# Transposing normalised tokens before their scale is known, with unused TensorE products between the stages

## What is computed

```python
def act_qdq(x):                       # one scale for the whole tensor
    scale = jnp.maximum(jnp.max(jnp.abs(x)) / qmax, 1e-12)
    return jnp.clip(jnp.round(x / scale), -qmax - 1.0, qmax) * scale

x = x + tanh(g_xattn[0]) * cross_attention(layernorm(x), ctx)      # "x2" below
h = layernorm(x)
h = act_qdq(h)
up, gate = act_qdq(h @ Wup.T), act_qdq(h @ Wgate.T)
sig  = fixed_qdq_u16(sigmoid(gate))
gate = act_qdq(gate * sig)
o    = act_qdq(gate * up)
x    = x + tanh(g_ffn[0]) * (o @ Wdown.T)
```

## Time and profile before

| | us |
|---|---|
| median of 3 runs | 591.79 (590.91 to 591.95) |
| the profiled execution's own time | 594.23 |
| its span in the trace | 592.1 |
| attention ends on PE | 432.2 |
| input maximum known (DVE reciprocal L1358) | 440.1 |
| first gate product | 445.6 |
| last gate tile copied out | 484.7 |
| all second-pass products done | 548.1 |
| first and last down product | 552.5 and 589.4 |

### The profile page before, as it was taken

How to read it: one execution, slowest core, us unless ns; L and a number is a source line. 1 busy time by engine, 2 the same in 40 slices (tenths; PEclk the granted TensorE clock), 3 DMA queues, 4 the chain that set the end, 5 groups by cost and what they waited for, 6 DMA issues and landing times. The chain is left out here.

```text
span 592.1 us, 10973 instructions
## 1 busy us (share of the span) xinstructions
PE 522.1 (88%) x3921; PEld 455.9 (77%) x3921; DVE 410.9 (69%) x1080; ACT 298.1 (50%) x859; POOL 123.4 (21%) x137
## 2 busy tenths in 40 slices
PE   2999999999999999999999999998738999900798
PEld 2888889888988988888898898886527888700698
DVE  4679844755674574576457458758676998999896
ACT  2734622543443353264335336426515559989992
POOL 3001310220231031022013012212223008940000
PEclk9999999999999999999999999999967999955699
DMA  7922001100110110110011001004000100010033
GB/s 248 359 105 73 1 1 54 37 2 19 35 35 0 53 35 0 53 35 0 0 53 35 0 2 37 2 1 159 2 18 1 38 0 1 0 35 1 1 106 107
DMA packets 18478, 25.86 MB, mean 44 GB/s; under 512 B 1216, under 2 KB 15808, under 8 KB 18448
## 3 DMA queue, kind: packets, MB, share of 16 engines
q1 hardware_dynamic: 18192, 25.17, 12.7%
q0 software_dynamic: 256, 0.30, 0.3%
HBM read 21.27 MB, written 4.19 MB: 43 GB/s over the span
## 5 line engine op out<-in xcount | busy, mean ns | idle before, releaser
L805 ACT ACTIVATE probs<-bank,nmax 128x129 f32<-128x129 f32 x256 | 90.7, 367 | 118.0 <-DVE nmax L1133 117.8
L1552 POOL TENSOR_TENSOR probs<-probs,rinv 128x512 f32<-128x512 f32 x64 | 66.6, 1041 | 338.8 <-DVE rinv L1141 338.8
L608 PE MATMUL bank<-wv,ctxT 128*128 128x512 f32 x384 | 94.3, 397 | 0.0
L600 PE MATMUL bank<-ctxT,wk 128*128 128x256 f32 x672 | 88.9, 282 | 0.0
L600 PEld LDWEIGHTS bank<-ctxT,wk 128*128 128x128 f32 x672 | 83.6, 188 | 0.0
L608 PEld LDWEIGHTS bank<-wv,ctxT 128*128 128x128 f32 x384 | 70.5, 188 | 16.9 <-issue 1.2
L1145 DVE COPY pT<-bank 128x512 f32<-128x512 f32 x64 | 43.7, 683 | 20.8 <-PE bank L671 18.7
L786 ACT ACTIVATE oT<-bank 128x256 fp32r<-128x256 f32 x64 | 24.7, 385 | 60.0 <-PE bank L680 60.0
L600 PE MATMUL bank<-xnT,wq 128*128 128x256 f32 x336 | 54.7, 298 | 0.0
L805 ACT ACTIVATION_READ_ACCUMULATOR probs<-bank,nmax 128x1 f32 x256 | 52.0, 203 | 0.0
L600 PEld LDWEIGHTS bank<-xnT,wq 128*128 128x128 f32 x336 | 43.2, 188 | 7.2 <-issue 1.2
(11 more groups left out here) (170 smaller groups left out, 814.6 us busy)
## 6 DMA issues: line engine op xcount, KB each, us to landing
craw<-in_ctx SPq DMA_DIRECT2D x8, 512.0 KB, 3.3
stage<-in_L_xattn_Wkv SPq DMA_DIRECT2D x8, 512.0 KB, 12.6
xa<-in_x SPq DMA_DIRECT2D x8, 256.0 KB, 2.7
xr<-in_x SPq DMA_DIRECT2D x8, 256.0 KB, 2.8
x_scratch<-y SPq DMA_DIRECT2D x7, 256.0 KB, 2.1
x2all<-x_scratch SPq DMA_DIRECT2D x1, 1792.0 KB, 7.8
xres<-x_scratch SPq DMA_DIRECT2D x6, 256.0 KB, 2.9
out<-yout SPq DMA_DIRECT2D x6, 256.0 KB, 2.2
```

Of the source, the lines that this page charges most:

```text
L600: last = mm(bk[:, n * TG:(n + 1) * TG], wt[a][:, k, f], act_t[b][:, k, :], start=(k == 0 and i == 0), stop=(k == kk - 1 and i == len(TERMS ...
L608: last = mm(bk[:, :], ctxT[a][:, k, b * S:(b + 1) * S], wv[w][:, k, h * 512:(h + 1) * 512], start=(k == 0 and i == 0), stop=(k == KC - 1 a ...
L805: last = nc.scalar.activation(probs[:, c % 2, u, 0:NK], score_bank[c % 2][h][:, b * QW:b * QW + NK], ACT.Exp, bias=nmax[:, c % 2, u:u + 1] ...
L1552: G.tensor_tensor(probs[:, c % 2, :, 0:S], probs[:, c % 2, :, 0:S], rinv[:, c % 2, :].rearrange("p (u o) -> p u o", o=1).to_broadcast([P, ...
```

## The change

- A first square root covers the 14 batches that are known before the last group ends (`root(0)`, started by DVE in the last attention unit F8), and a second one only the last two. There are now four roots instead of three.
- ACT normalises the tokens, x * (1/deviation) - mean/deviation, pair by pair, between the roots (`x_normalise`, pairs 0 to 6; pair 7 in the gate pass). PE transposes these normalised tokens, pairs 0 to 5 before the scale is known, each into a bank of its own (`x_bank`), pairs 6 and 7 after the first quarter of the gate pass.
- With the scale known, the transposed tokens are multiplied by its reciprocal straight out of the bank into int16: pairs 0 and 1 by DVE, the rest by ACT (`x_integers`). `fa[2]`, `x_float` and POOL's rounding are gone. The high part is made from the int16 tile. The low part of pairs 2 to 7 moves from DVE to POOL, for which ACT writes one more f32 copy (`xfloat`).
- DVE takes gate maxima and minima over two tiles at a time (`gate_range`).
- PE runs products whose results nobody reads (`keep_awake`, 128x512, into bank 7): 4 before `global_max(0)`, 7 after it; 4 after each of the products 4 to 11 of the second pass; 8 after `global_max(4)`.
- In the second pass DVE rounds chunk 7 instead of chunk 11.
- SP's read of the residuals waits for the last transposition instead of POOL's last rounding.

```diff
+            def keep_awake(count, rows, spare_bank):
+
+                for _ in range(count):
+                    mm(spare_bank[:, :], rows[:, 0:P], rows, start=True, stop=True)
...
             def x_transposes(t):
-                pe.wait_ge(xf_ready, t + 1)
-                if t >= 2:
-                    pe.wait_ge(xt_lo, t - 1)
+                last_pair = t == NT // 2 - 1
+                pe.wait_ge(xn2_ready, t + 1)
+                if t == 5:
+                    pe.wait_ge(x2_ready, NG)
+                if last_pair:
+                    pe.wait_ge(xi_scalar, 3)
...
+            for t in range(NT // 2 - 2):
+                x_transposes(t)
+            pe.wait_ge(x2_ready, NG + 1)
+            keep_awake(4, wg[0][:, 0, 0:512], bank[7])
             global_max(0)
-            for t in range(2):
-                x_transposes(t)
+            keep_awake(7, wg[0][:, 0, 0:512], bank[7])
...
-                        if m == 0 and tg == 0 and j in (1, 3):
-                            x_transposes(2 + j // 2)
...
-                    if m == 0 and tg < 2:
-                        x_transposes(2 * tg + 4)
-                        x_transposes(2 * tg + 5)
-            for n in range(2, 5):
+                    if m == 0 and tg == 0:
+                        x_transposes(NT // 2 - 2)
+                        x_transposes(NT // 2 - 1)
+            for n in range(2, 4):
                 global_max(n)
+            for q in range(4, NCH):
+                pe.wait_ge(o_ready, q)
+                keep_awake(4, down_rows, bank[7])
+            global_max(4)
+            keep_awake(8, down_rows, bank[7])
...
+            def x_normalise(t):
+                last_pair = t == NT // 2 - 1
+                if t == 0:
+                    act.wait_ge(x2all_in, 16)
+                if t == 0 or last_pair:
+                    act.wait_ge(xaffine, 2 if last_pair else 1)
+                for b in range(2):
+                    n = 2 * t + b
+                    last = nc.scalar.activation(xnlast[:, b, :] if last_pair else x2all[:, n, :], x2all[:, n, :],
+                                                ACT.Identity, bias=fa[:, 3, n:n + 1], scale=rs3[:, 0, n:n + 1])
+                last.then_inc(xn2_ready, 1)
+
+            root(0)
+            x_normalise(0)
+            root(1)
+            for t in range(1, 4):
+                x_normalise(t)
+            root(2)
+            for t in range(4, 6):
+                x_normalise(t)
+            root(3)
+            x_normalise(6)
...
             def x_high(t):
-                act.wait_ge(xt_done, t + 1)
-                high(xT[0][:, :, t * TG:(t + 1) * TG],
-                     unit_bank[t % 2][:, :].rearrange("p (k s) -> p k s", k=KD)).then_inc(xt_hi, 1)
+                if t < 2:
+                    act.wait_ge(xi_vector, t + 1)
+                else:
+                    act.wait_ge(xi_scalar, t - 1)
+                    high(xfloat(t), xi[:, t % 4, :, :])
+                high(xT[0][:, :, t * TG:(t + 1) * TG], xi[:, t % 4, :, :]).then_inc(xt_hi, 1)
...
+            x_high(0)
+            x_high(1)
+            x_integers(2)
+            x_integers(3)
+            x_high(2)
+            x_high(3)
+            for n in range(4 * KI):
+                gu(0, n)
+                if n in (1, 2, 7, 8):
+                    t = {1: 4, 2: 5, 7: 6, 8: 7}[n]
+                    x_integers(t)
+                    x_high(t)
+                if n == 3:
+                    x_normalise(NT // 2 - 1)
...
             link(V.reciprocal(s1(5), s1(4)))
-            link(V.tensor_scalar(fa[:, 2, :], rs3[:, 0, :], s1(5), None, ALU.mult))
...
-            V.memset(pause[:, :], 0.0).then_inc(xaffine, 1)
...
+            for t in range(2):
+                dve.wait_ge(xt_done, t + 1)
+                V.tensor_scalar(xi[:, t, :, :], x_bank[t][:, :].rearrange("p (k s) -> p k s", k=KD), s1(5), None,
+                                ALU.mult).then_inc(xi_vector, 1)
+            x_offsets(slice(known, NT))
...
+            def gate_range(n):
+
                 tg, j = n // KI, n % KI
...
+                dve.wait_ge(gu_out, n + 2)
+                src = gate[:, j:j + 2, tg * 512:(tg + 1) * 512]
+                V.tensor_reduce(amax[:, 0, n:n + 2], src, AX.X, ALU.max)
+                return V.tensor_reduce(amax[:, 0, 4 * KI + n:4 * KI + n + 2], src, AX.X, ALU.min, negate=True)
...
+            for t in range(2, NT // 2):
+                pool.wait_ge(xt_hi, t + 1)
+                hi = xT[0][:, :, t * TG:(t + 1) * TG]
+                G.tensor_tensor(xT[1][:, :, t * TG:(t + 1) * TG], xfloat(t), hi.bitcast(F32),
+                                ALU.subtract).then_inc(xt_lo_pool, 1)
```

More of the change, by code:

```diff
@@ L304, in gated_cross_attention_ffn @@
         unit_bank = [bank[6], bank[7]]
+        x_bank = [bank[i] for i in (2, 3, 4, 5, 1, 6, 7, 1)]
         stage_in = [sem(f"stage_in{i}") for i in range(NST)]
@@ L428, in gate_by_vector @@
         def gate_by_vector(q):
[L430 removed]
+            return q in (3, 7)
         def gate_rounded(engine, q):
@@ L871, in _, with root @@
             nc.scalar.activation(spare[:, :], ident[:, 0:1], ACT.Sqrt)
-            for k in range(3):
+            known = NT - GB
+            def root(k):
                 act.wait_ge(root_in, k + 1)
-                var, out_root = (rs3[:, 1, :], rs3[:, 2, :]) if k == 2 else (rs[:, 5, k:k + 1], rs[:, 6, k:k + 1])
-                nc.scalar.activation(out_root, var, ACT.Sqrt).then_inc(root_out, 1)
[L877 to L881, removed]
@@ L1223, in _, with link, s1, scale_of_row @@
             dve.wait_ge(const_ready, 1)
+            last2 = x2all[:, (NG - 1) * GB:, :]
+            known = NT - GB
+            fc = [9]
+            def link(ins):
+                fc[0] += 1
+                ins.then_inc(fchain, 1)
+                dve.wait_ge(fchain, fc[0])
+            def s1(i):
+                return small[:, i:i + 1]
+            def scale_of_row(n, s, factor_q):
+                dve.wait_ge(gm_1, n + 1)
+                link(V.tensor_scalar(row[:, :], bank[0][:, 0:P], factor_q, MIN_SCALE, ALU.mult, ALU.max,
+                                     accum_out=s1(s)))
+            def root_start(var, r, eps):
+                V.tensor_scalar(r[1], var, eps, None, ALU.add).then_inc(root_in, 1)
+            def root_end(k, r):
+                dve.wait_ge(root_out, k + 1)
+                link(V.reciprocal(r[0], r[2]))
+                newton(link, r)
+            def last_range(b):
+                n = (NG - 1) * GB + b
+                V.tensor_reduce(x2_max[:, n:n + 1], last2[:, b, :], AX.X, ALU.max)
+                return V.tensor_reduce(x2_min[:, n:n + 1], last2[:, b, :], AX.X, ALU.min)
+            def root_columns(cols):
+                return [rs3[:, i, cols] for i in range(3)]
+            def x_offsets(cols):
+                V.scalar_tensor_tensor(out=fa[:, 3, cols], in0=mean_var[:, cols, 0], scalar=-1.0,
+                                       in1=rs3[:, 0, cols], op0=ALU.mult, op1=ALU.mult).then_inc(xaffine, 1)
             def group(g):
@@ L1358, in _ @@
             link(V.reciprocal(s1(5), s1(4)))
-            link(V.tensor_scalar(fa[:, 2, :], rs3[:, 0, :], s1(5), None, ALU.mult))
-            link(V.scalar_tensor_tensor(out=fa[:, 3, :], in0=mean_var[:, :, 0], scalar=-1.0, in1=fa[:, 2, :],
-                                        op0=ALU.mult, op1=ALU.mult))
-            V.memset(pause[:, :], 0.0).then_inc(xaffine, 1)
-            dve.wait_ge(x2all_in, 16)
-            for b in range(2):
-                last = V.tensor_scalar(xi[:, 0, b, :], x2all[:, b, :], fa[:, 2, b:b + 1], fa[:, 3, b:b + 1],
-                                       ALU.mult, ALU.add)
@@ L1399, in _ @@
                 x_low(t)
-            for n in range(4 * KI):
-                last = gu_maximum(0, n)
-                if n in (1, 3):
-                    x_low(2 + n // 2)
-                if n in (KI - 1, 2 * KI - 1):
-                    x_low(4 + 2 * (n // KI))
-                    x_low(5 + 2 * (n // KI))
+            for n in range(0, 4 * KI, 2):
+                last = gate_range(n)
             link(last)
```

123 lines of the change are left out of this document (50 added, 73 removed).

## The result

| kernel | median us | range | ratio to before on the same chip, 95% |
|---|---|---|---|
| before | 591.74 | 590.75 to 592.85 | |
| changed | 588.07 | 586.81 to 588.59 | 0.9928 (0.9911 to 0.9946) |

The changed kernel is faster by 3.7 us here, about half of the 7.0 of the sum. The profiled execution's own time is 588.16, its span 586.1.

The account below looks back on a forecast made before the run. Bounds were taken stage by stage: a DVE-ACT-PE chain, PE, POOL, DVE, then PE's down products, with PE's clock halved in two places. Terms -2.8 - 4.4 + 1.0 + 0 - 0.8 = -7.0 gave 584.8 us, range 583.0 to 588.4.

Parts of the forecast that it names:

- the sum: All five parts added: -7.0 us, taken from the median 591.79 to give 584.8.
- What bounds: DVE-ACT-PE chain before the gate, PE in gate pass, POOL in up pass, DVE in second pass, PE in down products.
- part 1: From the input maximum to the first gate product: -2.8 us, bounds -2.2 and -3.2.
- the third: Rival: each change between root and `Identity` loads a table, 1.28 us, delaying DVE; 589.4 us, chance 0.02.
- fourth rival: `x_normalise` is so slow that the roots are late; 593.6 us at 1.35 us each, chance 0.02.
- Part 2: Gate pass: full clock from the start and fewer transpositions, 38.46 to 34.1 us, -4.4.
- Part 3: Gate maximum over two tiles at a time starts only with the last tile: +1.0 us, bounds 0.9 and 1.3.
- Part 4: Second pass: DVE stays the bound, 0 us, bounds -0.2 and +0.4; the clock comes back within it.
- second rival: Clock does not come back in the second pass, so `global_max(4)` is held up: 587.6 us, chance 0.07.
- Part 5: Down pass at full clock from the start, DVE the next bound: -0.8 us, bounds 0 and -2.0.
- The range: 583.0 to 588.4 us, holding the likeliest case and the first two rivals.
- first rival: Clock falls in gaps before the gate pass; 2.9 us there and 0.2 come back: 587.9 us, chance 0.17.

Follow-up runs that it names:

- combined kernel: Changed kernel with second rounding on POOL, last two gate tiles one at a time, pairs 6 and 7 one tile later: 585.92 us, ratio 0.9881.
- second trace of before: The kernel before, no edit, profiled and timed again: 592.22 us, ratio 0.9999, span 588.8.
- two later comparisons: The changed kernel, no edit, timed twice more beside the kernel before: 586.84 us, ratio 0.9906, and 587.34 us, ratio 0.9915.
- gaps filled: Combined kernel with more unused products, POOL rounding only after the second pass's products, first piece on DVE: 584.12 us, ratio 0.9873.
- third trace of the changed kernel: The changed kernel, no edit, in the second of its two repeats: 587.34 us, ratio 0.9915.

## Why the prediction was right, and its size too large

**What bounds, and part 1: right.** The stage went from 13.37 to 10.55 us, 2.8 as worked out. The high parts ran on ACT beside DVE, and two low parts back to back took 1.29 us. No root was late: 591 ns for the new operation, where 0.6 was estimated. No table load stands between roots and `Identity`: the trace has three loads, at 0.75, 426.26 and 478.20. That rules out the third and the fourth rival.

**Part 2: right, small miss, then mis-based.** The clock was 1.00 throughout and the pass took 34.41 us against 34.1; the wait for pair 7 was 0.29 us against 0.5. Taken from the 38.46 of the shown trace this is 4.05. Taken from the 37.76 of the second it is 3.36, because there the half-clock stretch was 4.2 us and not 5.8.

**Part 3: right.** 3.74 to 4.75 us, +1.01; PE waited 0.80 us for the maximum, where 0.9 was estimated. With only the last two tiles taken singly 0.35 came back, since the double length of the pair before them still made DVE late (combined kernel).

**Part 4: right.** 24.75 and 24.77 us; the clock came back in the pass at about 535. The second rival did not happen in any trace.

**Part 5: right bound, smaller gain.** DVE became the bound as the chain shows, and the pass went from 36.96 to 36.34, 0.6 where 0.8 was taken; from the second trace of before only 0.2.

**The step that made the sum too large** is the first sentence of the method: the sum was made as a difference within one profiled execution and subtracted from the median of others. That execution's own time was 594.23, 2.4 above the median, and I carried all 7.0 over, though two terms, parts 2 and 5, hung on how long the clock stayed down in it. Set against that same trace the change gave 157.2 to 150.8, -6.4: here part 2 was taken 0.3 and part 5 0.2 too large. Set against the second trace it reads -2.8 - 3.4 + 1.0 + 0 - 0.2 = -5.4 (156.1 to 150.7), and the two later comparisons gave -5.7 and -5.1. About half of the executions of the kernel before are of either kind by their mean clock, so neither trace alone is the right base. The range covered it: 588.07 lies 0.3 under its upper end, which is little room.

**What remains open** is the first comparison's -3.7. Its interval, 3.2 to 5.3 us, overlaps those of the two repeats (3.8 to 7.3 and 3.7 to 6.3), so that part of the difference may be chance. The clock does not account for it: the mean granted clock of the six timed executions was 0.9785 in the first comparison, 0.9778 and 0.9783 in the others. Of the six only the profiled one has a trace. It was 1.4 and 1.6 us longer than those of the repeats, and 1.2 and 1.4 of this were there at the first attention output copy already (58.23 against 56.99 and 56.82). For the other executions nothing shows where the time went.

From that copy to the end of attention 13 of the 14 traces took 374.3 or 374.4 us. The one that took 376.7 is that with the rounding on POOL and no unused products in the second pass, where the clock was down within attention:

```profile
422.30:429.10 6.80, 6.24 (x32) 5.51 (x30) 4.79 (x13) 3.51 (x7) 0.00 (x0) 0.50 0.00 0
```

So the clock is not held in every execution, in code that the change does not touch either.

**A warning in the numbers.** The first rival gave 587.9, and 588.07 was measured. By the total one would say that it had come true. The windows say that in this trace it had not: the clock was 1.00 in the whole gap and in the gate pass, and so it was in the traces of both repeats. That the total fell on the rival's number is coincidence.

## What to carry to other kernels

Before a difference read in one trace is subtracted from a median, take a second trace of the same kernel and see which terms change. Here those changed that hang on how long the clock stays down and on how long the first weights take to arrive. Unused products paid where PE was the next bound (about 2 us at the gate pass, 1.1 in a down pass relieved of DVE) and were worth nothing that could be timed where another engine was the bound just behind it. Ask of each gain what is next late, and relieve that in the same step: the down pass went 36.96, 36.33, 35.17 as the clock and then DVE were dealt with, and 34.85 with the gaps filled as well.

## What the runs showed of the hardware that was not expected

- DVE's product of two int16 tensors took 1.62 to 1.64 us in three of five cases beside POOL's roundings, and 1.22 otherwise; POOL's roundings took 0.69 us for the first and 2.72 for the last two. With POOL's roundings put behind the products the second pass went from 25.69 to 24.90 us. The Trainium skill (SBUF — State Buffer, Who interferes with whom) states that a DVE instruction with two inputs in SBUF contends with a GpSimd instruction that reads SBUF; the trace agrees, and the waiting seen here is 0.4 us on three of DVE's instructions and up to 2.0 on one of POOL's.
- The clock does not fall in every execution after the same gap. It gave way to 0.50 for about 3.4 us in five places, each in a gap of 1.6 to 2.0 us on PE or within 0.9 us behind it: at 442.8 in the kernel with the rounding on POOL, at 439.8 and 549.0 in the kernel before with unused products, at 546.4 in the third trace of the changed kernel and at 547.2 in the kernel without unused products at the gate. In the first trace of the changed kernel the same gap of 1.88 us before the first gate product left it at 1.00. What decides it was not found.
- So PE busy without a gap can still be granted less than full speed: 3.00 of 3.00 us at 0.63 in the kernel before with unused products, 3.30 of 3.30 at 0.53 in the down pass of the third trace.
